# A one-core decoder layer: large elementwise work moved off GpSimd, and a new order by hand on ScalarE, VectorE and TensorE

## What is computed

```python
x = x + attn(layernorm(x), ...)      # down to 64 channels, rmsnorm, two window attentions, up, gelu ffn
x = x + xattn(ctx, layernorm(x), Wq) # k = v = ctx Wq^T; causal softmax over 1024 tokens
x = x + ffn(layernorm(x), ...)       # a shared expert and 8 routed ones, top 2 of 8

# attn, on X = layernorm(x)
xi = rmsnorm(X @ down_w + down_b)
o1 = branch(xi[:, :32], window 10, shift 5); o2 = branch(xi[:, 32:], window 20, shift 10)   # 8 heads of 4
y = X + concat(o1, o2) @ up_w + up_b
return y + gelu(rmsnorm(y) @ ffn_w1 + ffn_b1) @ ffn_w2 + ffn_b2

# ffn, on X = layernorm(x): every expert is computed for every token
h1 = gelu(einsum('td,edh->teh', X, rw1) + rb1)
mixed = einsum('ted,te->td', einsum('teh,ehd->ted', h1, rw2) + rb2, weights)
return gelu(X @ sw1 + sb1) @ sw2 + sb2 + mixed
```

## Time and profile before

| what | value |
| --- | --- |
| median of 3 runs | 169.75 us (167.92 to 173.85) |
| profiled execution, whole | 169.46 us |
| its span, first to last instruction | 167.7 us |
| mean granted TensorE clock | 0.98 of full speed |
| PE, DVE, ACT, POOL busy | 92%, 84%, 62%, 31% |
| moved from and to HBM | 9.47 MB read, 0.56 MB written |

### The profile page before, as it was taken

The page is one execution under the profiler, slowest core; times in us unless marked ns, Lnnn a source line. Parts: engine busy times, 40 slices in busy tenths (PEclk is TensorE's granted clock), DMA queues, the critical chain, the costliest instruction groups (busy, mean ns, idle before and its releaser), DMA issues.

```text
span 167.7 us, 3154 instructions
## 1 busy us (share of the span) xinstructions
PE 154.4 (92%) x1121; PEld 117.6 (70%) x1121; DVE 140.4 (84%) x250; ACT 103.7 (62%) x186; POOL 51.3 (31%) x62
## 2 busy tenths in 40 slices
PE   0799999999999997999859999999999999999992
PEld 0737875659996566799646767787788778887861
DVE  3886899999996999986889368999888894999972
ACT  3104276521283572575956877995997689989641
POOL 7589999100000996004270030030514000000000
PEclk9999999999999999999975999999999999999999
DMA  5999100000000000000000039300000004721002
GB/s 159 358 281 416 49 4 0 6 4 0 0 0 0 4 2 0 0 0 4 0 2 0 2 103 279 127 0 0 2 4 0 0 0 150 265 96 39 24 0 63
DMA packets 5233, 10.23 MB, mean 61 GB/s; under 512 B 627, under 2 KB 2287, under 8 KB 4962
## 3 DMA queue, kind: packets, MB, share of 16 engines
q1 hardware_dynamic: 4902, 9.74, 17.5%
q10 hardware_dynamic: 316, 0.29, 0.6%
HBM read 9.47 MB, written 0.56 MB: 60 GB/s over the span
## 4 chain that ended last, share of the span: by engine, by line
PE 71%; DVE 16%; issue 4%; DMA 2%; ACT 2%; POOL 2%; POOLq 1%; DVEq 0%; ACTq 0%
PE ps L1530 64%; PE ps L1814 3%; DVE room L1173 2%; DMA x_sb<-in_x 2%; DVE xf_lo L1297 2%; PE ps L1594 2%; DVE room L1180 1%; DVE st L1076 1%; POOLq L94 1%; DVE room L1358 1%; POOL rstd L582 1%; POOL rstd L580 1%; DVE xcT L1210 1%; DVE room L1070 1%; PE ps L1728 1%
## 5 line engine op out<-in xcount | busy, mean ns | idle before, releaser
L1370 DVE TENSOR_TENSOR low<-room,high 128x1024 fp32r<-128x1024 f32 (+1 forms) x20 | 22.1, 1114 | 4.0 <-ACT high L902 3.7
L886 ACT ACTIVATE room<-ps,consts_sb 128x512 f32<-128x512 f32 x36 | 23.3, 681 | 1.6 <-PE ps L1530 1.0
L902 ACT ACTIVATE high<-room 128x1024 fp32r<-128x1024 f32 (+1 forms) x20 | 19.1, 970 | 4.0 <-PE ps L1530 2.4
L580 POOL TENSOR_SCALAR rstd<-mv 128x1 f32<-128x1 f32 (+4 forms) x13 | 5.5, 425 | 46.4 <-DVE mv L1281 31.1
L1530 PE MATMUL ps<-xf_lo,w_hi 128*128 128x512 f32 x36 | 15.2, 422 | 1.7 <-DVE xf_lo L1297 1.7
L1530 PE MATMUL ps<-xf_hi,w_hi 128*128 128x512 f32 x36 | 16.7, 464 | 0.0
L592 POOL TENSOR_SCALAR xn<-x_sb,mv,rstd 128x128 f32<-128x128 f32 x8 | 16.2, 2033 | 0.0
L1358 DVE TENSOR_TENSOR room<-room,gates 128x1024 f32<-128x1024 f32 (+1 forms) x13 | 14.7, 1137 | 0.7 <-ACT room L886 0.7
L582 POOL TENSOR_TENSOR rstd<-rstd,minus_half 128x1 f32<-128x1 f32 (+4 forms) x18 | 14.7, 817 | 1.9
L1530 PE MATMUL ps<-high,w_hi 128*128 128x512 f32 x36 | 14.6, 406 | 0.0
L1530 PE MATMUL ps<-xf_hi,w_lo 128*128 128x512 f32 x36 | 14.6, 405 | 0.0
(11 more groups left out here) (211 smaller groups left out, 371.2 us busy)
## 6 DMA issues: line engine op xcount, KB each, us to landing
gates<-gate_rows SPq DMA_DIRECT2D x12, 256.0 KB, 5.8
...
```

The source lines that it names most:

```text
L580: step(pool.tensor_scalar(dst, src, scale, eps, ALU.mult, ALU.add))
L886: act.activation(hidden_at(q), ps[:, z_bank(q), :], ACT.Gelu, bias=cols_sb[:, i:i + 1]).then_inc(moe_h_ready, 1)
L902: act.activation(split_part(high, h, e, a, z), hidden_part(h, e, a, z), ACT.Copy).then_inc(high_ready, 1)
L1370: dve.tensor_tensor(split_part(low, h, e, a, z), hidden_part(h, e, a, z), split_part(high, h, e, a, z).bitcast(F32), ALU.subtract).then_in ...
```

## The change

Four parts.

1. POOL keeps only vectors with a few elements a partition, and its clearing of buffers. The normalised x goes to ACT: POOL makes `x_shift`, minus mean times 1/std (`xn_shift`, two small instructions), and eight `xn_tile(t)` on ACT compute x times 1/std plus `x_shift`. The two casts of `narrow` go to ACT. The three `xs_add` go to DVE. `clear` moves behind `rstd1_pow(1)`.
2. Four more fillers of the kind `idle_joined` (47 in place of 43), all between the last transposes of `xf_columns` and the first expert products, and one of them between two products; six of the old fillers now stand ahead of PE's first matmul.
3. `gelu_table`, one tiny Gelu that loads the table, moves from the second half's experts to behind `hT_copy(0, 0)`.
4. A new order of the calls on ACT, DVE and PE all along.

```diff
-            def xn_tiles():
+            def xn_shift():
                 pool.wait_ge(rstd0_ready, 2)
-                for t in range(NT):
-                    pool.tensor_scalar(xn[:, t, :], x_sb[:, t, :], mv[:, t, 0:1], rstd0[:, t:t + 1],
-                                       ALU.subtract, ALU.mult).then_inc(xn_ready, 1)
+                step(pool.tensor_tensor(x_shift[:], mv[:, :, 0], rstd0[:], ALU.mult))
+                settle()
+                pool.tensor_scalar(x_shift[:], x_shift[:], -1.0, None, ALU.mult).then_inc(x_shift_ready, 1)
...
             rstd0_pow(0)
-            clear()
             rstd0_pow(1)
             rstd1_pow(0)
+            xn_shift()
             rstd1_pow(1)
-            xn_tiles()
+            clear()
             rstd2_pow(0, 0)
             rstd2_pow(0, 1)
-            xs_add(0, 0)
-            xs_add(0, 1)
-            narrow()
             rstd3_pow(0, 0)
...
+            def narrow():
+                act.wait_ge(ld_down, 16)
+                act.activation(ident16[:], ident, ACT.Copy).then_inc(casts, 1)
+                act.wait_ge(ld_late, 16)
+                act.activation(causal16[:], causal_sb, ACT.Copy).then_inc(casts, 1)
+
+            def xn_tile(t):
+                act.wait_ge(x_shift_ready, 1)
+                act.activation(xn[:, t, :], x_sb[:, t, :], ACT.Identity, bias=x_shift[:, t:t + 1],
+                               scale=rstd0[:, t:t + 1]).then_inc(xn_ready, 1)
...
             window_cols(0, 0)
+            narrow()
+            wqc_copy()
             qkv_copy(1, 0)
             window_cols(0, 1)
+            xn_tile(0)
+            w1_high()
             window_cols(1, 1)
...
             hT_copy(0, 0)
-            hT_copy(0, 1)
+            gelu_table()
             ffn_gelu(0, 0, 0)
             ffn_gelu(0, 1, 0)
+            hT_copy(0, 1)
...
             xc20_copy(1)
-            w2_high()
+            xn_tile(7)
+            pT_copy(3)
             xf_high(0, 0)
             xfT_copy(0, 0)
             xfT_copy(0, 1)
+            xp_squares(1, 0)
             xf_high(0, 1)
-            xp_squares(1, 0)
...
+            def xs_add(h, k):
+
+                a, z = PIECES[h][k]
+                hs = slice(h * TH + a, h * TH + z)
+                dve.wait_ge(xs_begun, 1)
+                dve.wait_ge(xp_ready, h * TH + z)
+                dve.tensor_tensor(xs[:, hs, :], xs[:, hs, :], xp[h][:, a:z, :], ALU.add).then_inc(xs_ready, z - a)
...
             window_weighted(1, 1)
+            x1_moments(0, 0)
             value_add(1, 1)
-            x1_moments(0, 0)
+            row_max(0)
+            xs_add(0, 1)
```

346 lines of the change are left out of this document (172 added, 174 removed).

## The result

| | before | changed |
|---|---|---|
| median, us (runs) | 170.58 (4) | 175.18 (4) |
| lowest to highest | 167.92 to 173.85 | 173.97 to 175.62 |
| profiled execution, span | 167.7 | 171.8 |
| third product of the first expert tile starts | 86.61 | 92.34 |
| from there to the end of the span | 81.1 | 79.5 |

The mean granted clock of the four runs was .95, .931, .941 and .941. The ratio is 1.036, with a 95% interval of 1.023 to 1.050. The mean granted clock of a kernel differs from one execution to the next, and so does its time: intervals leave out runs more than 1.5% above the fastest of their kernel, medians are over all runs. Of the ten runs of the changed kernel in both measurements, nine lie at .92 to .95 and 173.7 to 175.9 us, and one at .979 took 169.32, a time that before has too.

The account below looks back on a forecast made before the run. DVE's chain bounds the kernel until 86.61 us, then PE. Path -2.0, clock -3.0, fillers +0.4 and experts' order +0.4 sum to -4.2: 165.3 us, 165.6 against the median; range 163.3 to 167.3, with rivals 163.2 to 170.0.

Parts of the forecast that it names:

- (g): Clock ahead of the experts: added fillers keep it up where before worked 6.0 us at the lower level; -3.0 us.
- slower than before: Rival, 12%: POOL's small instructions wait out two-input DVE instructions and become last on the path; 172.6 us.
- The rival whose clock does not hold: Rival, 25%: the path shortens but the clock still falls ahead of the experts; 168.3 us, against the median 168.6.
- a 5 in the clock row: Sign of being wrong: a slice of the profile page's clock row shows the clock at its lower level.
- (a): Start of the kernel: window margins in DVE's wait for x and six fillers ahead of the first matmul; -0.4 us.
- (b): Normalised x from POOL to ACT, 0.29 us a tile: five DVE window products run without POOL beside them; -0.2 us.
- (c): DVE's values(1, 0) and value_add(1, 0) moved earlier: waits for the branch-20 output and the values shrink; -1.1 us.
- (d): xs_add(0, 0) and (0, 1) on DVE: +0.8 us on the path, while two DVE losses beside POOL go, -1.06.
- (e): POOL's rstd3_pow waits out value_add(1, 1) on DVE, delaying row_max(0); +0.6 us, between 0 and +2.2.
- (f): Ahead of the experts: w2_low(0) earlier and xf_low(0, 0) without POOL, -2.0 us; xf_high(0, 1) behind ACT's squares, +1.1.
- (h): Experts' stage: two fillers inside it, +0.4 us, and the new order of products, +0.4, between 0 and +3.

Follow-up runs that it names:

- e1: Changed kernel with its six leading fillers moved behind qkv_rows(1, 0) and between the halves of qkv_rows(1, 1): median 171.87 us.
- e6: Changed kernel with eleven more fillers behind qkv_rows(1, 0), in qkv_rows(0, 0) and among the 160 small products: median 174.0 us.
- e18: Changed kernel without its six leading fillers, nothing in their place: median 173.58 us, ratio to before 1.001.
- e9: Changed kernel with window_product(1, 1) put back ahead of window_values(1, 0) on DVE: median 174.66 us.
- e10: Changed kernel with the eleven added fillers of e6 and window_product(1, 1) put back ahead of window_values(1, 0): median 171.83 us, ratio to before 1.014.
- e11: e10 with value_add(1, 1) put back ahead of x1_moments(0, 0) on DVE: median 174.03 us, ratio to before 1.015.
- e8: Before, order kept, with casts and xn on ACT, xs_add on DVE, and the changed fillers ahead of the experts: median 169.15 us, ratio 0.991.
- e4: Before in its own order with casts and xn moved to ACT and xs_add to DVE: median 169.59 us, ratio 0.985.
- e14: Before with the 160 small products of branch 1's second half in one piece ahead of keys(0): median 174.3 us.
- e15: Before with branch 0's second-half products ahead of scores and value sums; scores and one filler also leave the small products: median 173.42 us.
- e3: Before with only the changed kernel's fillers ahead of the experts: median 168.29 us, ratio 0.985.

## Why the prediction was wrong, by its own steps

**The step that failed is (g), by what it left out.** It priced the clock in one place, ahead of the experts, because that was the only fall in the one profile that I had, and all the other terms took PE's durations at full rate. Its own first paragraph noted that before the experts PE is padded with products on zeros, and it did not ask what the reordering did to that padding. The change put six fillers at the front, cut those behind `qkv_rows(1, 0)` from four to two, and joined the 160 small products of `qkv_rows(1, 1)` into one piece, where a product of scores and two fillers had parted them. The term that was missing is the clock ahead of 80 us, put at nothing without a reason: the clock was at 1.2 GHz for 17 us there, and DVE's waits for PE grew by 6.8 us. e1's run at .998, 6.8 us under the changed kernel's median, and e6's third product, at least 4.7 us earlier, say the same.

The range ended at 170.0 and no rival covered this case. The rival "slower than before" had the sign right by luck: it blamed GpSimd's answers, for the first of which DVE waited 0.59 us where it feared 2.2. The rival whose clock does not hold is nearer in kind, but looked only ahead of the experts, where the clock held. Of the signs of being wrong, "a 5 in the clock row" came true.

Without the falls, how far off was the sum? e1's run at .998 has a span of 165.5 us; less the 79.5 of the rest, the third product would begin at an estimated 86.0, so the path gained some 0.6 us and not 2.0, a little more if the three fillers that e1 has among its small products are taken off. Which term of the path fell short stays open, since no trace has this order at full clock without fillers added. Behind the third product, (g) was too large, as told below.

(a) was right and small: DVE's first `window_product` began at 17.68 instead of 18.51, -0.8 against -0.4 forecast. The leading fillers are not shown to be dear later on: e18, without them, lost the clock in seven of twelve runs all the same.

(b) was right in effect: it began after the same wait and took 3.49 us instead of 3.53. But an `xn` activation, with its scale and shift from memory, takes 0.48 us (in ScalarE's timeline), not the 0.29 of the square:

```profile
18.49 0.48 ACT L709 ACTIVATE xn<-x_sb,x_shift,rstd 128x128 f32<-128x128 f32 x1
```

The Trainium skill ("ScalarE: Activation LUTs", section "What ACT_TABLE_LOAD costs") has 186 ns plus 0.833 ns an element plus some 93 ns for each operand given by pointer, which is an estimate of 0.48 us for two; the trace agrees.

(c) is the nearer theory for that swap (e9, e10), but its -1.1 us did not come in this trace: `xc_add(0)` was due near 50 and ran at 56.89, and at 43 to 49 us PE, at half clock, ends last. In e6, at full clock, it ran at 52.19, of which the six fillers among the small products took 2.0; so it would have been near 50 without them, an estimate and not a run.

(d) was right to a tenth: 0.42 us each, `window_weighted(1, 1)` 3.48, as the earlier trace rows had it without POOL beside it.

(e) was right in size: the wait is 0.59 us. The 0.6 of the forecast was a value picked between 0 and 2.2, so that is part luck, and that the wait is a loss at all, e11 doesn't confirm.

(f) was right in its parts: `xf_low(0, 0)` 0.56, the wait of PE for it next to nothing. What came late behind it was not ACT's squares but the router's product on PE, for which DVE waited 1.02 us at 91.41. e8 shows 1.2 us from `xf_low` and from the rest of the moved work.

(g) was right where it looked, 1.00 from 84 to 94 us, though e4, e14 and e15 show that the clock can stay up there without the added fillers. It was over-priced: 81.1 - 79.5 = 1.6 us gained and not 3.0. From the third product to the next expert's first, before took 6.3 us (86.61 to 92.93) and e3 4.7 (86.45 to 91.15): not half, since PE waits 0.4 us there at full clock, and four transposes took 0.78 us where they had taken 0.70 at half clock.

(h): the rest of the span is 79.5 us in the changed kernel, with one filler more behind the third product (the other stands ahead of it), and 79.5 in e3 and e4 with the old expert order, in e4 with no filler more. Neither the new order nor the filler shows there, where the forecast had 0.8.

At an equal clock little speaks against the change: its run at .979 took 169.32, five of e18 at .965 to .98 took 169.0 to 170.0, while before took 169.9 to 175.2, in the middle 170.8, in its 15 runs at .978 to .98. At full clock e1's 167.64 stands beside before's 167.91 and 168.56. So the path looks shorter by some 0.3 to 1 us, by single runs, and the clock takes back more than that.

**What stays open.** Which arrangement inside the later list lowers the clock: e14 (the joined small products) is the stronger of the two moves, but with four runs each, and e14's profile holds falls that its move can't have brought. No kernel with the changed list held the clock in all of its runs. Nor is it shown that the fillers' places alone decide: e1 changes the start and the middle at once, and e6, with eleven more, was at .941 to .96 in three of four. Why the first rise comes at 12 us in some executions and at 14 in others was not tried. Before's own runs at .96 to .97, 37 of 76, must have falls that its profile does not show; where, no trace here says.
